# Vision-transformer tower, encoder phases: two first products in alternation, the up weights' low part split in halves, the variance amid the values, row factors spread by a transpose

## What is computed

```python
for l in range(LAYERS):
    keys = jnp.concatenate([past, x], axis=1)
    q = (x @ Wq.T + bq).reshape(B, T, HEADS, HEAD_DIM)
    k = (keys @ Wk.T + bk).reshape(B, T + H, HEADS, HEAD_DIM)
    v = (keys @ Wv.T + bv).reshape(B, T + H, HEADS, HEAD_DIM)
    ...
    attn = jax.nn.softmax(scores, axis=-1)
    o = jnp.einsum('bhqk,bkhd->bqhd', attn, v).reshape(B, T, C)
    o = o @ Wo[l].T + bo[l]
    x = _ln(x + o, ln1_g[l], ln1_b[l])
    ff = jax.nn.gelu(x @ W1[l].T + b1[l], approximate=False) @ W2[l].T + b2[l]
    x = _ln(x + ff, ln2_g[l], ln2_b[l])
```

## Time and profile before

| | us |
|---|---|
| median of 3 runs | 890.88 (888.78 to 891.69) |
| the profiled execution, its own time | 893.74 |
| its span, first to last instruction | 891.9 |
| encoder phases with x and y, 382.8 to 798 | 415.2 |
| PE busy / DVE / ACT / POOL | 818.8 / 641.0 / 462.9 / 257.0 |

### The profile page before, as it was taken

The page is one execution under the profiler, slowest core; times in us unless marked ns, Lnnn a source line. Parts: engine busy times, 40 slices in busy tenths (PEclk is TensorE's granted clock), DMA queues, the critical chain, the costliest instruction groups (busy, mean ns, idle before and its releaser), DMA issues.

```text
span 891.9 us, 16181 instructions
## 1 busy us (share of the span) xinstructions
PE 818.8 (92%) x5846; PEld 752.1 (84%) x5846; DVE 641.0 (72%) x1274; ACT 462.9 (52%) x823; POOL 257.0 (29%) x297
## 2 busy tenths in 40 slices
PE   6977799999999999799989999999998999989788
PEld 4877676999999998798979989898897989879456
DVE  5656149388888885777787877878788787875686
ACT  3363331443333335566767577567676756744421
POOL 0003010041111110245264155435515524532132
PEclk9978769999999998899999999999999999998989
DMA  5000092698888862010110021021002102010000
GB/s 174 1 1 1 31 401 54 240 317 316 316 317 320 319 214 98 1 37 14 48 50 33 12 94 35 12 93 36 0 19 87 35 12 94 22 76 1 1 0 28
DMA packets 18288, 88.33 MB, mean 99 GB/s; under 512 B 3120, under 2 KB 7472, under 8 KB 12240
## 3 DMA queue, kind: packets, MB, share of 16 engines
q1 hardware_dynamic: 18256, 87.90, 27.9%
HBM read 85.05 MB, written 2.84 MB: 99 GB/s over the span
## 4 chain that ended last, share of the span: by engine, by line
PE 42%; issue 26%; POOL 18%; DVE 9%; ACT 4%; DMA 0%; POOLq 0%; SPq 0%; DVEq 0%; ACTq 0%
PE bank L1064 13%; POOL W_L L1866 6%; PE bank L1101 5%; POOL arena L1851 4%; POOL HF_L L1910 4%; PE bank L1206 2%; PE bank L770 2%; POOL WQKV_L L1866 2%; PE bank L1110 2%; PE bank L724 2%; POOL SQ L1880 2%; PE bank L1382 2%; PE bank L733 1%; PE bank L1047 1%; PE bank L917 1%
## 5 line engine op out<-in xcount | busy, mean ns | idle before, releaser
L1064 PE MATMUL bank<-arena 128*128 (+1 forms) x1024 | 117.9, 274 | 0.5 <-ACT arena L1609 0.5
L1064 PEld LDWEIGHTS bank<-arena 128*128 128x128 f32 x1024 | 117.4, 192 | 0.7 <-ACT arena L1609 0.7
L1851 POOL TENSOR_TENSOR arena<-arena,srec 111x456 f32<-111x456 f32 x56 | 52.4, 963 | 144.1 <-DVE srec L2010 144.1
L770 PE MATMUL bank<-XHL,W_H 128*128 128x296 f32 x384 | 89.2, 311 | 0.0
L770 PE MATMUL bank<-XHL,WQKV_H 128*128 128x296 f32 x288 | 74.0, 330 | 5.8 <-DVE XHL L2391 4.9
L1910 POOL TENSOR_TENSOR HF_L<-arena,HF_H 128x296 fp32r<-128x296 f32 x48 | 43.9, 937 | 114.1 <-ACT HF_H L1766 114.1
L1866 POOL TENSOR_TENSOR W_L<-LW,W_H 128x256 fp32r<-128x256 f32 x96 | 70.1, 767 | 18.9 <-ACT W_H L1652 18.9
L770 PEld LDWEIGHTS bank<-XHL,W_H 128*128 128x128 f32 x384 | 65.2, 191 | 0.7
L770 PEld LDWEIGHTS bank<-XHL,WQKV_H 128*128 128x128 f32 x288 | 50.1, 196 | 12.7 <-DVE XHL L2391 7.9
L2022 DVE TENSOR_SCALAR OB<-bank,lvec 96x148 f32<-96x148 f32 x144 | 51.2, 368 | 12.9 <-PE bank L840 10.6
L1766 ACT ACTIVATE arena<-bank,vec 128x296 f32<-128x296 f32 x96 | 48.9, 509 | 22.5 <-PE bank L770 22.3
(11 more groups left out here) (251 smaller groups left out, 2121.5 us busy)
## 6 DMA issues: line engine op xcount, KB each, us to landing
arena<-ew_in SPq DMA_DIRECT2D x16, 2048.0 KB, 9.4
arena<-ew_in SPq DMA_DIRECT2D x16, 1024.0 KB, 6.8
LW<-lw_in SPq DMA_DIRECT2D x12, 1024.0 KB, 4.9
arena<-route SPq DMA_DIRECT2D x32, 185.0 KB, 3.5
LW<-lw_in SPq DMA_DIRECT2D x6, 768.0 KB, 4.3
fp_weights<-arena SPq DMA_DIRECT2D x1, 2048.0 KB, 6.4
arena<-fp_weights SPq DMA_DIRECT2D x1, 2048.0 KB, 7.2
arena<-patches_in SPq DMA_DIRECT2D x2, 864.0 KB, 8.1
```

What stands on the lines that cost most here:

```text
L770: last = mm(o, w, x, start=(i == 0), stop=(i == len(pairs) - 1))
L1064: last = mm(o[:, m * CAP:(m + 1) * CAP], w[:, kc, mi * P:(mi + 1) * P], xg(kc, e), start=(kc == 0), stop=(kc == C - 1))
L1851: nc.gpsimd.tensor_tensor(v, v, srec[0:QROWS, s:s + 2, :].unsqueeze(3).to_broadcast([QROWS, 2, C * JH, KEYS]), ALU.mult).then_inc(p_ready, 1)
```

## The change

It has five parts. (1) The first two products of a half, of values and of up, are issued together by `two_products`: all eight matmuls on XH into two banks, then the four on XL. (2) The second `values` of a phase is cut: its first chunk comes before the variance, its second after. (3) The row factors are spread by three transposes of 128 by 128. (4) POOL splits W1 no longer at the end of the phase before but in the phase that uses it: four pieces once the stream of that phase is complete (`x_ready`), then SQ, then the other four, then W2. (5) In `down` the last three hidden chunks are finished for output chunk 0 before output chunk 1.

```diff
--- before.py
+++ after.py
@@ -729,9 +729,9 @@
                 pe.wait_ge(ln_rstd, ln_count(seq, h))
-                for t, (t0, n) in enumerate(var_tiles(nt)):
-                    last = mm(ln_bank(seq, h)[:, t0 + P - n:t0 + P], ln_rs[:, h, t:t + 1].to_broadcast([P, P]),
-                              ident[:, P - n:P], start=True, stop=True)
+                for t, (t0, _) in enumerate(var_tiles(nt)):
+                    last = nc.tensor.transpose(ln_bank(seq, h)[:, t0:t0 + P], ln_rs[:, h, t:t + 1].to_broadcast([P, P]),
+                                               ident)
                 last.then_inc(ln_bcast, 1)
@@ -760,23 +760,32 @@
-            def products(o, pairs, high_count=None, low_count=None):
+            def products(o, pairs):
                 for i, (w, x) in enumerate(pairs):
-                    if high_count is not None and i < 2 * C and i % 2 == 0:
-                        pe.wait_ge(xh_ready, chunk_count(high_count, i // 2))
-                    if low_count is not None and i == 2 * C:
-                        pe.wait_ge(x_ready, low_count)
                     last = mm(o, w, x, start=(i == 0), stop=(i == len(pairs) - 1))
...
-            def project_v(r, plan, h, pairs, high_count=None, low_count=None):
-                for c in range(C):
-                    key = ("w", 2 * h + c)
-                    free_bank(r, plan, key)
-                    products(bank_of(plan, key)[:, 0:NHALF], pairs(c), high_count if c == 0 else None,
-                             low_count if c == 0 else None).then_inc(filled["w"], 1)
+            def two_products(r, plan, keys, pairs, high_count, low_count):
+                for part in range(2):
+                    for key, all_pairs in zip(keys, pairs):
+                        o = bank_of(plan, key)[:, 0:NHALF]
+                        if part == 0:
+                            free_bank(r, plan, key)
+                        for i in (range(2 * C) if part == 0 else range(2 * C, 3 * C)):
+                            if key is keys[0] and part == 0 and i % 2 == 0:
+                                pe.wait_ge(xh_ready, chunk_count(high_count, i // 2))
+                            if key is keys[0] and i == 2 * C:
+                                pe.wait_ge(x_ready, low_count)
+                            last = mm(o, *all_pairs[i], start=(i == 0), stop=(i == 3 * C - 1))
+                        if part == 1:
+                            last.then_inc(filled[key[0]], 1)
+            def project_v(r, plan, h, pairs, high_count, low_count):
+                two_products(r, plan, [("w", 2 * h + c) for c in range(C)], [pairs(c) for c in range(C)],
+                             high_count, low_count)
@@ -826,10 +835,10 @@
-            def values(r, plan, g4):
+            def values(r, plan, g4, chunks=range(C)):
                 h = g4 // 2
-                for c in range(C):
+                for c in chunks:
                     key = ("o", 2 * g4 + c)
@@ -1216,15 +1225,20 @@
+                    def up_pairs(m):
+                        return stream_pairs("w1", slice(m * P, (m + 1) * P), hy)
                     def up(*ms):
...
                             free_bank(ry, plan, key)
-                            cols = slice(m * P, (m + 1) * P)
-                            products(bank_of(plan, key)[:, 0:NHALF], stream_pairs("w1", cols, hy),
-                                     xa_count(ly, hy, 0) - skipped(ly, hy, 0) if m == 0 else None,
-                                     x_count(ly, hy, 0) - skipped(ly, hy, 0) if m == 0 else None
-                                     ).then_inc(filled["f1"], 1)
+                            products(bank_of(plan, key)[:, 0:NHALF], up_pairs(m)).then_inc(filled["f1"], 1)
+                    def up_first():
+                        two_products(ry, plan, [("f1", FM * hy + m) for m in range(2)], [up_pairs(m) for m in range(2)],
+                                     xa_count(ly, hy, 0) - skipped(ly, hy, 0),
+                                     x_count(ly, hy, 0) - skipped(ly, hy, 0))
@@ -1232,18 +1246,20 @@
                             free_bank(ry, plan, key)
-                        for m in range(FM):
-                            if m < FM // 2:
+                        tail = FM - 3
+                        order = [(m, c) for m in range(tail) for c in range(C)]
+                        order += [(m, c) for c in range(C) for m in range(tail, FM)]
+                        for m, c in order:
+                            if c == 0 and m < FM // 2:
                                 pe.wait_ge(hl_ready, low_count_of(ly, hy, m))
-                            else:
+                            elif c == 0:
                                 pe.wait_ge(hl_ready_pool, low_count_of(ly, hy, m - FM // 2))
-                            for c in range(C):
-                                parts = three("w2", m, slice(c * P, (c + 1) * P), HF_H[:, m, :], HF_L[:, m, :])
-                                for i, (w, moving) in enumerate(parts):
-                                    last = mm(bank_of(plan, keys[c])[:, 0:NHALF], w, moving,
-                                              start=(m == 0 and i == 0), stop=(m == FM - 1 and i == 2))
-                                if m == FM - 1:
-                                    last.then_inc(filled["f2"], 1)
+                            parts = three("w2", m, slice(c * P, (c + 1) * P), HF_H[:, m, :], HF_L[:, m, :])
+                            for i, (w, moving) in enumerate(parts):
+                                last = mm(bank_of(plan, keys[c])[:, 0:NHALF], w, moving,
+                                          start=(m == 0 and i == 0), stop=(m == FM - 1 and i == 2))
+                            if m == FM - 1:
+                                last.then_inc(filled["f2"], 1)
@@ -1296,7 +1312,9 @@
                 for i in range(4):
-                    if y:
+                    if y and i == 0:
+                        up_first()
+                    elif y:
                         up(2 * i, 2 * i + 1)
@@ -1319,10 +1337,12 @@
                     gate_up(0, 0)
+                if x and y:
+                    values(rx, plan, 2 * hx + 1, (0,))
                 if y:
...
                 if x:
-                    values(rx, plan, 2 * hx + 1)
+                    values(rx, plan, 2 * hx + 1, (1,) if y else range(C))
                 else:
@@ -1857,14 +1877,18 @@
+            def split_part(name, lo, hi):
+                value, high, low = (t.rearrange("p c n -> p (c n)") for t in SPLIT[name][:3])
+                for at in range(lo, hi, LOW_COLS):
+                    cols = slice(at, at + LOW_COLS)
+                    last = nc.gpsimd.tensor_tensor(low[:, cols], value[:, cols], high[:, cols], ALU.subtract)
+                return last
             def split_weights(name, l):
-                value, high, low = (t.rearrange("p c n -> p (c n)") for t in SPLIT[name][:3])
                 pool.wait_ge(wh_ready[name], l + 1)
-                for lo in range(0, value.shape[1], LOW_COLS):
-                    cols = slice(lo, lo + LOW_COLS)
-                    last = nc.gpsimd.tensor_tensor(low[:, cols], value[:, cols], high[:, cols], ALU.subtract)
-                last.then_inc(wl_ready[name], 1)
+                split_part(name, 0, C * 3 * D if name == "qkv" else 2 * FM * P).then_inc(wl_ready[name], 1)
@@ -1899,9 +1923,14 @@
+                if y and y[0] == 0:
+                    pool.wait_ge(wh_ready["w1"], y[1] + 1)
+                    pool.wait_ge(x_ready, y[1] * 4 + 4)
+                    split_part("w1", 0, FM * P)
                 if y:
...
                     if y[0] == 0:
+                        split_part("w1", FM * P, 2 * FM * P).then_inc(wl_ready["w1"], 1)
                         split_weights("w2", y[1])
@@ -1915,7 +1944,7 @@
                     add_squares(y[1], 1, y[0])
-                if late_split(x):
+                if late_split(x) and late_split(x)[0] == "qkv":
                     split_weights(*late_split(x))
```

## The result

The changed kernel takes **874.73 us** (874.52 to 879.32, four runs), the kernel before 890.68 beside it: ratio 0.9836, 95% interval 0.9808 to 0.9864. So it gained 14.6 us (12.1 to 17.1), where 8.9 was forecast. The absolute time lies 1.3 us under the range's low end; by the ratio, on 890.88, it is 876.3, at that end. Ratios leave out executions more than 1.5% above the fastest of the same kernel: two of the six of the kernel without part 5, none elsewhere. Run again beside other kernels the changed one took 876.98 us (875.1 to 877.53, six runs), ratio 0.9854 (0.9827 to 0.9882). The profiled execution took 874.68 us, against 893.74 before.

What follows compares the result with a forecast made beforehand. It took DVE's chain at phase borders and middles to bound the kernel, PE only filling in. Terms -4.8 - 6.0 - 3.8 + 5.7 = -8.9 us, set on 890.88, gave 882.0 us, range 876 to 887.

Steps and rivals of the forecast that it cites:

- The frame: Border between encoder phases: a chain over DVE; PE only fills in and earns nothing unless DVE starts sooner.
- The likeliest case: The forecast itself, collision of XL with the W2 split included: 882.0 us, chance 61%.
- Part 2: Values chunk before the variance: DVE's idle time before gathering goes, -0.44 us in each of eleven phases, -4.8 us.
- Part 3: Row factors by transposes: -0.30 us in twelve phase middles, nothing at borders, -1.5 before the encoder; -6.0 with the tail.
- The tail's 0.9 us: Last phase and tail: three more transposed row factors on a path where engines wait for each other, -0.9 us.
- Part 4 at the border: Five borders: XL no longer beside the W1 split, RSUM meeting a piece; -0.75 us each, -3.8 us.
- The collision: Middle of six phases: XL of the first norm meets the W2 split, +0.95 us each, +5.7 us.
- No collision: Rival, 15%: XL of the first norm escapes the W2 split or DVE has slack; the 5.7 go, 876.3 us.
- The gathering not sooner: Rival, 13%: at phase ends the extra values delay the variance by more than the bank saves; 886.8 us.
- The borders giving nothing: Rival, 6%: encoder borders only move waits between engines, the collision comes, transposes pay for it; -0.3 us, 890.6 us.
- The clock falling at the borders: Rival, 5%: more transposes and waits at borders lower the granted clock, costing 16 us; 898 us.
- The signs named ahead: Trace signs: XL 0.53 us an operation at borders, 1.0 in kind A; PE's SQ wait gone; kind B 0.74 us shorter.

Runs made afterwards that it cites:

- the kernel without part 5: The changed kernel with the down products going chunk by chunk to the end again: 881.6 us, ratio 0.9863 (six runs).
- Part 4 alone: The kernel before with only the W1 split in halves behind the stream: 891.97 us, ratio 1.0008 (ten runs).
- the two profiles with both waits: The changed kernel with W2's split held for XL of the first norm and W1's first pieces for RSUM: 871.97 us, run again 873.79 us.
- part 2 alone: The kernel before with only one chunk of the second values ahead of the variance: 883.47 us, ratio 0.991 (four runs).
- the transposes outside: The kernel before with transposes only in the norms outside the encoder's layers: 886.52 us, ratio 0.9958 (twelve runs).

## Why the prediction was right, and where its terms were off

**The frame held.** The border is a chain over DVE; PE's moves alone gave nothing (part 1 at 0 in all phases, part 5 at 0 from the 13th RSUM on); the variance, the transposes and XL gave, because DVE started sooner. The likeliest case came true, collision included, but the gain was larger than its own spread of 879.5 to 884.5 allowed. The range reached the measurement only by the ratio (876.3 us, against its end at 876) and only with the end that a rival gave it, a rival that did not come: that it held was luck.

**Part 2: mis-sized, -6.9 for -4.8.** The step that failed was taking the idle time of the gathering's row, 0.51 us, for all there was to win, and then taking 0.07 off. Idle time is counted from the reciprocal's end. Back to back, DVE starts the next operation 0.09 us ahead of that end (443.92 + 0.18 = 444.10, gathering at 444.01). So 0.51 us of idle time are 0.60 of cadence. And the 0.07 was not paid: before, the variance stood 0.05 us behind SQ's end (450.69 + 0.81, 451.55), now 0.07 (441.89 + 0.81, 442.77). I had used this very overlap for PE, 0.16 us, and not for DVE.

**Part 3: right where it was isolated.** 0.24 to 0.29 us in each middle for 0.30, nothing at the borders. Ahead of the encoder one pair of profiles gives 1.7 us for 1.5, but the two norms behind 336 us give as much by themselves, and the other six are open. The tail's 0.9 us is open: in the profiles the tail varied from 89.9 to 93.5 us with the clock, and no run isolates it.

**Part 4 at the border: right.** XL 0.97 us for two, RSUM 0.79 to 1.0 with a piece at its start for the 0.9 assumed, 0.71 us won for 0.75. SQ, W1's low part and the first up product were in time, as argued.

**The collision: the mechanism right, the size not, +3.3 for +5.7.** Both operations were priced at the full 0.95 us. Part 4 alone showed that price; in the changed kernel the first operation met a piece's end. That an operation could also lose several pieces at once, as twice without part 5, was not foreseen, and it lies outside the bound of 5.8 us that was taken from the longest operation of the kernel before. My own terms had the 0.30 us by which the transposes move XL against POOL, but I used it only to ask whether XL would meet the split, not where in a piece. In the changed kernel's profile the bounds of 0 and 5.8 did hold it.

**The sum.** -8.9, with -2.1 for part 2 and -2.4 for the collision, is -13.4, against 14.6 and 13.0 measured. The two mis-sized terms had opposite signs in the sum and the same sign in error.

**The rivals.** No collision: refuted by XL at 1.51 us. The gathering not sooner: refuted. The borders giving nothing: refuted by 10.2 us. The clock falling at the borders: from 374 to 780 us it is 1.00, and so in every variant, but for 3.4 us from 473.1 on in the profile without part 5, where PE had just stood 2.19 us for the late XL. The signs named ahead came true, save that only one of XL's two operations took 1.0 us; a phase of kind B is 0.9 us shorter instead of 0.74, and one of kind A 1.1 instead of 0.5.

## What to carry to other kernels

Ask of each step which engine's cadence it shortens: work moved into a waiting engine's gap was free here, and worth nothing unless the engine that sets the end starts sooner. Read gains on that engine from start to start, since idle time between records hides the overlap that back-to-back operations have. Where VectorE's operations on two SBUF tiles meet a stream of GpSimd pieces, hold the pieces behind the operation with a semaphore, if the pieces have slack: two such waits were worth 5.5 us here, over half of what the whole change won in these phases, and in the two profiles with both waits no XL or RSUM operation meets a piece any more.

## What was not expected of the hardware

**An operation waits for the piece, and rarely for the stream.** Beside POOL an XL or RSUM operation ends 0.32 us after the piece that it meets, wherever it starts in it; so it costs anything from nothing to 0.5 us, and 0.27 us of shift elsewhere decides it. Twice, in the kernel without part 5, it ended 0.32 us after the fourth piece behind the one that it met, and cost 2.8 us. POOL's piece pays too, 0.96 us in place of 0.72. R and XD, which read one operand from PSUM, keep their 0.95 us for two beside the same pieces (XD at 457.33); the small COPY of `lvec` takes 0.70 instead of 0.17.

**The clock ahead of and behind the encoder differs between executions of one program.** The 57 runs of the kernel before that stand beside the experiments lie between 886.69 us at a mean clock of 0.970 and 894.94 at 0.957, and a line through them falls by 0.57 us for each 0.001, with 0.8 us left over. Taken to one clock by that line, which is an estimate and takes out what a change does by way of the clock, part 2 alone stands at -7.2 us (encoder -7.1), part 4 alone at +2.0 (+2.3), the transposes outside at -1.9 (-1.7 ahead), the changed kernel's second set at -13.6. Of that, 10.2 is the encoder and some 1.7 what lies ahead; 1.7 are left for the tail, where 1.2 was forecast and nothing isolates it. A gain of a few us in such a kernel should be read from a stage at full clock and not from two spans.
